# A fused cross-attention and mixture-of-experts layer: the closing loads and stores take four or five neighbouring token rows per partition, and the shared tiles follow in steps of four columns

## What is computed

```python
x = x + xattn(layernorm(x), ctx)        # q, k, v from layernorms, softmax over 361 keys, output product
h = layernorm(x)
shared = gelu(h @ ws1 + bs1) @ ws2 + bs2
aff = softmax(h @ Wr + br)              # 31 experts
vals, idx = top_k(aff, 3)               # a gate for each of the three experts of a token
routed = sum over experts e: gate_e * (gelu(h @ We1[e] + Be1[e]) @ We2[e] + Be2[e])
out = x + shared + routed + h
```

## Time and profile before

| | |
|---|---|
| median of 3 runs | 559.9 us (558.31 to 562.15) |
| the profiled execution, its own time | 565.31 us |
| its span, first to last instruction | 563.7 us |
| TensorE busy | 494.3 us (88%) |
| VectorE busy | 349.2 us (62%) |
| GpSimd busy | 323.2 us (57%) |
| ScalarE busy | 248.2 us (44%) |
| mean granted TensorE clock | 0.958 |
| moved by DMA | 97.53 MB, mean 173 GB/s |

### The profile page before, as it was taken

One profiled execution on the slowest core, in us unless ns is written; L12 is line 12 of the kernel. 1 busy time (PEld: TensorE's weight loads), 2 busy tenths in 40 slices (PEclk: granted clock), 3 DMA queues, 4 the chain that ended last, 5 costly groups with the idle time before them and its releaser, 6 DMA issues.

```text
span 563.7 us, 15096 instructions
## 1 busy us (share of the span) xinstructions
PE 494.3 (88%) x3227; PEld 416.7 (74%) x3228; DVE 349.2 (62%) x1531; ACT 248.2 (44%) x822; POOL 323.2 (57%) x366
## 2 busy tenths in 40 slices
PE   1789888899989988879739999999999999999990
PEld 1777777777777777667528888888888888898760
DVE  2368797878888895443206666666666666663385
ACT  1154566555656556351205444444444444453210
POOL 5032666766775676354106777777777777786000
PEclk9989999999999999787959999999999999999995
DMA  8975677677664422189335887777877887786899
GB/s 248 300 220 161 208 227 251 209 212 225 191 198 137 148 87 87 68 282 375 137 86 90 131 122 125 124 126 127 125 129 126 129 125 126 128 127 74 269 348 315
DMA packets 80618, 97.53 MB, mean 173 GB/s; under 512 B 8401, under 2 KB 65394, under 8 KB 80578
## 3 DMA queue, kind: packets, MB, share of 16 engines
q1 hardware_dynamic: 60146, 70.52, 40.9%
q0 software_dynamic: 19568, 25.88, 27.6%
q10 hardware_dynamic: 864, 0.66, 0.4%
HBM read 55.31 MB, written 41.73 MB: 172 GB/s over the span
## 4 chain that ended last, share of the span: by engine, by line
PE 41%; SPq 10%; issue 6%; POOL 4%; DMA 3%; DVE 3%; ACT 2%; POOLq 0%; DVEq 0%; ACTq 0%
PE bank L1133 15%; PE bank L1122 15%; PE bank L1111 4%; POOL sum L508 3%; SPq L372 2%; SPq L368 2%; DMA w_all<-sum 2%; SPq L399 1%; SPq L398 1%; SPq L373 1%; PE bank L982 1%; SPq L400 1%; DMA sum<-y_sb,token 1%; PE bank L985 1%; PE bank L1032 1%
## 5 line engine op out<-in xcount | busy, mean ns | idle before, releaser
L508 POOL DMA_INDIRECT sum<-y_sb,token x105 | 170.7, 1626 | 73.5 <-issue 63.9
L593 ACT ACTIVATE up<-bank,b_all 128x128 f32<-128x128 f32 x260 | 81.5, 364 | 117.4 <-PE bank L1122 66.8
L1133 PE MATMUL bank<-w_all,up 128*128 x420 | 113.1, 392 | 0.6 <-issue 0.4
L1122 PE MATMUL bank<-xtt,w1b 128*128 128x128 f32 x840 | 112.9, 278 | 0.2
L1122 PEld LDWEIGHTS bank<-xtt,w1b 128*128 128x128 f32 x840 | 102.9, 193 | 3.1 <-issue 2.9
L482 POOL DMA_INDIRECT expert_rows_in<-xt,slot x75 | 74.4, 992 | 35.5 <-issue 31.5
L856 DVE TENSOR_SCALAR y_sb<-bank,gate,inverse 128x256 f32<-128x256 f32 x105 | 57.1, 544 | 42.6 <-PE bank L1133 37.9
L1133 PEld LDWEIGHTS bank<-w_all,up 128*128 128x128 f32 x420 | 71.4, 190 | 10.9 <-issue 1.8
L848 DVE COPY w1b<-w_all 128x512 f32 x105 | 45.2, 430 | 41.4 <-PE bank L1122 37.7
L619 ACT ACTIVATE xtt<-bank 128x256 f32<-128x256 f32 x105 | 40.3, 384 | 59.4 <-PE bank L1111 33.4
L1111 PE MATMUL bank<-ident,xt 128*128 128x128 f32 x210 | 40.7, 276 | 11.9 <-DMA xt<-expert_rows_in 11.9
(11 more groups left out here) (183 smaller groups left out, 904.0 us busy)
## 6 DMA issues: line engine op xcount, KB each, us to landing
xt<-expert_rows_in SPq DMA_DIRECT2D x105, 132.0 KB
w_all<-in_w SPq DMA_DIRECT2D x43, 256.0 KB, 9.7
w_all<-in_ctx SPq DMA_DIRECT2D x32, 288.0 KB
w_all<-sum SPq DMA_DIRECT2D x12, 512.0 KB, 8.9
w_all<-sum SPq DMA_DIRECT2D x9, 384.0 KB, 8.2
sum<-pad_rows SPq DMA_DIRECT2D x1, 3328.0 KB, 12.4
w_all<-in_w SPq DMA_DIRECT2D x1, 3328.0 KB
w_all<-in_x SPq DMA_DIRECT2D x25, 128.0 KB, 3.4
```

The source lines that it names most:

```text
L508: pool.indirect_dma_start(sums[s], bass.IndirectOffsetOnAxis(ap=token[sx][:, 0:1], axis=0), y_sb[sx][:, :], None, compute_op=ALU.add).then ...
L593: ins = act.activation(up[s][:, m * P:m * P + P], up_ps[s][:, m * P:m * P + P], ACT.Gelu, bias=b1_all[:, e, m:m + 1].rearrange("p o n -> p ...
L1122: mm = pe.matmul(up_ps[s][:, m * P:m * P + P], w[:, c * INTER + m * P:c * INTER + m * P + P], xtt[s][:, c * P:c * P + P], start=(c == 0), ...
L1133: mm = pe.matmul(down_ps[s], up[s][:, m * P:m * P + P], w, start=(m == 0), stop=(m == 1))
```

## The change

It has five parts, all of which follow from one new rule: in a group of tiles `lo` to `hi`, partition p now holds the hi - lo neighbouring tokens from lo * 128 + p * (hi - lo) on, so that a group's rows are four (in one group five) neighbouring rows of DRAM for each partition.

1. The layout: `rows_of` is rearranged as "(p k) n -> p k n". A tile t of the shared expert is now the columns `every(t)` of `tok`, 128 columns at a step of 4 (of 5 in one group), where it was 128 neighbouring columns. This holds for the right-hand side of `up_shared`, for the gates in `down_shared`, for the output of `evac_shared` and for the read of `tok` in the closing addition. `up_shared` waits for `h_t_copied` of the whole group.
2. The groups: six of 4, 4, 4, 4, 5 and 4 tiles, where there were seven of 3, 4, 3, 4, 3, 4 and 4. So 18 loads and 6 stores in place of 21 and 7; the bytes are the same. The last group is tiles 8 to 11, where it was tiles 21 to 24.
3. The gates: one transpose of 32 columns per tile (25) in place of 7 of 128 columns, into one row of 3200 columns in 32 partitions; 7 copies on ScalarE in place of 2. The copies alternate between two PSUM banks, so some transposes wait for a copy.
4. The order: copies 1 and 2 and their transposes stand in steps 33 and 34; the last four rounds follow each other after `early(5)`; ScalarE's copies for them stand one gelu earlier (`u == 6`).
5. At the start: `b2_all` is loaded once in place of four times, and one memset goes.

```diff
-GROUPS = [(12, 15), (0, 4), (15, 18), (4, 8), (18, 21), (8, 12), (21, 25)]
+GROUPS = [(12, 16), (0, 4), (16, 20), (4, 8), (20, 25), (8, 12)]
+GATES = [(0, 4), (4, 8), (8, 12), (12, 16), (16, 20), (20, 24), (24, 25)]
...
-        gates_all = sb("gates_all", [P, 28, NE + 1])
-        gates_t = sb("gates_t", [P, 7, P])
+        gates_all = sb("gates_all", [P, TILES, NE + 1])
+        gates_t = sb("gates_t", [NE + 1, TOKENS])
...
+        group_of = {t: g for g in GROUPS for t in range(*g)}
+
+        def every(t):
+
+            lo, hi = group_of[t]
+            return slice(lo * P + t - lo, hi * P, hi - lo)
...
+        def gates_ps(r):
+            lo, hi = GATES[r]
+            return bank[7 if r in (4, 6) else 6][0:NE + 1, 0:(hi - lo) * P]
...
-                return dram[lo * P:hi * P, :].rearrange("(k p) n -> p k n", p=P)
+                return dram[lo * P:hi * P, :].rearrange("(p k) n -> p k n", p=P)
...
-            for q in range(4):
-                pool.dma_start(b2_all[q * 32:q * 32 + NE + 1, :], b2).then_inc(small_in, 16)
+            pool.dma_start(b2_all[:, :], b2).then_inc(small_in, 16)
...
+            def copy_gates(r):
+                lo, hi = GATES[r]
+                act.wait_ge(gates_transposed, r + 1)
+                act.activation(gates_t[:, lo * P:hi * P], gates_ps(r), ACT.Copy).then_inc(gates_t_copied, 1)
+
             for i in STEPS:
                 if i == B + 1:
-                    act.wait_ge(gates_transposed, 4)
-                    act.activation(gates_t[:, 0:4, :].rearrange("p g q -> p (g q)"), bank[6][:, :], ACT.Copy).then_inc(gates_t_copied, 1)
+                    copy_gates(0)
                 step(i)
                 if i == B + 1:
                     gelu_shared(0)
                     gelu_shared(1)
+                    copy_gates(1)
+                if i == B + 2:
+                    copy_gates(2)
             for u in range(2, S_E):
                 gelu_shared(u)
-                if u == 7:
-                    act.wait_ge(gates_transposed, 7)
-                    act.activation(gates_t[:, 4:7, :].rearrange("p g q -> p (g q)"), bank[7][:, 0:3 * P],
-                                   ACT.Copy).then_inc(gates_t_copied, 1)
+                if u == 6:
+                    for r in range(3, len(GATES)):
+                        copy_gates(r)
...
-                dve.tensor_copy(tok[:, :, cut(u)], down_ps[u % 2].rearrange("p (c q) -> p c q", c=2)).then_inc(y_made, 1)
+                dve.tensor_copy(tok[:, :, every(u)], down_ps[u % 2].rearrange("p (c q) -> p c q", c=2)).then_inc(y_made, 1)
...
-                    dve.tensor_tensor(rows, rows, tok[:, :, lo * P:hi * P].rearrange("p c (k q) -> p k c q", q=P),
+                    dve.tensor_tensor(rows, rows, tok[:, :, lo * P:hi * P].rearrange("p c (q k) -> p k c q", q=P),
...
-                pe.wait_ge(h_t_copied, t + 1)
+                pe.wait_ge(h_t_copied, group_of[t][1])
...
-                                       tok[:, c, cut(t)], start=(c == 0), stop=(c == 1))
+                                       tok[:, c, every(t)], start=(c == 0), stop=(c == 1))
...
-                pe.wait_ge(gates_t_copied, 1 if t < 16 else 2)
+                pe.wait_ge(gates_t_copied, min(len(GATES), (group_of[t][1] + 3) // 4))
...
-                pe.matmul(to, gates_t[q:q + NE + 1, t // 4, :], b2_all[q:q + NE + 1, :], start=False, stop=True)\
+                pe.matmul(to, gates_t[:, every(t)], b2_all[:, :], start=False, stop=True)\
...
+            def turn_gates(r):
+                lo, hi = GATES[r]
+                pe.wait_ge(gates_made, hi)
+                if r in (1, 2, 3, 5, 6):
+                    pe.wait_ge(gates_t_copied, {1: 1, 2: 2, 3: 3, 5: 4, 6: 5}[r])
+                for t in range(lo, hi):
+                    mm = pe.transpose(gates_ps(r)[:, (t - lo) * P:(t - lo + 1) * P], gates_all[:, t, :], ident[:, :])
+                mm.then_inc(gates_transposed, 1)
```

More of the change, by code:

```diff
@@ L149, in program @@
         b1_all = sb("b1_all", [P, NE + 1, 2])
-        b2_all = sb("b2_all", [P, D1])
+        b2_all = sb("b2_all", [NE + 1, D1])
         ident = sb("ident", [P, P])
         ones, tri = sb("ones", [P, P], BF16), sb("tri", [P, P], BF16)
-        gates_all = sb("gates_all", [P, 28, NE + 1])
-        gates_t = sb("gates_t", [P, 7, P])
+        gates_all = sb("gates_all", [P, TILES, NE + 1])
+        gates_t = sb("gates_t", [NE + 1, TOKENS])
         iota_slot, iota_e, tile_no = sb("iota_slot", [P, NE]), sb("iota_e", [P, NE]), sb("tile_no", [P, 1])
@@ L266, in program @@
         sum_made, final_made, final_out = sems("sum_made", "final_made", "final_out")
-        MADE = 22
+        MADE = 21
         LATE = 18
@@ L441, in _ @@
                             allow_small_or_imprecise_dtypes=True))
-            const(pool.memset(gates_all[:, 0:TILES, NE:NE + 1], 1.0))
-            k = const(pool.memset(gates_all[:, TILES:28, :], 0.0))
+            k = const(pool.memset(gates_all[:, 0:TILES, NE:NE + 1], 1.0))
             assert k == MADE, k
@@ L800, in _ @@
             dve.tensor_tensor(fold_o1[D2B:D2C, 0:D1], fold_o1[D2B:D2C, 0:D1], bo_row[D2B:D2C, :], ALU.add).then_inc(folds_ready, 1)
-            dve.wait_ge(small_in, 16 * 7)
+            dve.wait_ge(small_in, 16 * 4)
             for i in STEPS[2:]:
@@ L953, in _ @@
             pe.wait_ge(folds_ready, 1)
-            pe.wait_ge(small_in, 16 * 7)
+            pe.wait_ge(small_in, 16 * 4)
             def step(i):
@@ L1042, in up_shared @@
                         mm = pe.matmul(up_ps[s][:, m * P:m * P + P], w1_all[:, NE, c * INTER + m * P:c * INTER + m * P + P],
-                                       tok[:, c, cut(t)], start=(c == 0), stop=(c == 1))
+                                       tok[:, c, every(t)], start=(c == 0), stop=(c == 1))
                 mm.then_inc(up_made, 1)
             def down_shared(u, t, to):
-                s, q = u % 2, 32 * (t % 4)
+                s = u % 2
                 pe.wait_ge(act_made, u + 1)
-                pe.wait_ge(gates_t_copied, 1 if t < 16 else 2)
+                pe.wait_ge(gates_t_copied, min(len(GATES), (group_of[t][1] + 3) // 4))
                 for m in range(2):
                     pe.matmul(to, up[s][:, m * P:m * P + P], w2_all[:, NE, m * D1:(m + 1) * D1], start=(m == 0), stop=False)
-                pe.matmul(to, gates_t[q:q + NE + 1, t // 4, :], b2_all[q:q + NE + 1, :], start=False, stop=True)\
+                pe.matmul(to, gates_t[:, every(t)], b2_all[:, :], start=False, stop=True)\
                   .then_inc(down_made, 1)
@@ L1059, in early @@
                 down_shared(u, u, down_ps[u % 2])
-            def turn_gates(lo, hi, to):
-                pe.wait_ge(gates_made, min(TILES, 4 * hi))
-                for g in range(lo, hi):
-                    pe.transpose(to[:, (g - lo) * P:(g - lo + 1) * P], gates_all[:, 4 * g:4 * g + 4, :].rearrange("p k e -> p (k e)"),
-                                 ident[:, :]).then_inc(gates_transposed, 1)
+            def turn_gates(r):
[6 more added lines that the diff above has]
+                mm.then_inc(gates_transposed, 1)
             for i in STEPS:
@@ L1070, in _ @@
                     pe.wait_ge(shared_in, 32)
-                    turn_gates(0, 4, bank[6])
+                    turn_gates(0)
                 step(i)
@@ L1078, in _ @@
                     early(0)
+                    turn_gates(1)
                 if i == B + 2:
@@ L1081, in _ @@
                     early(1)
+                    turn_gates(2)
             pe.wait_ge(msum_made, TILES)
@@ L1096, in _ @@
             pe.wait_ge(logit_sum, TILES)
-            turn_gates(4, 7, bank[7])
+            for r in range(3, len(GATES)):
+                turn_gates(r)
             for u in range(7, S_E):
```

## The result

Timed in turn on one chip, the kernel took 561.02 us before (median of 4 runs, 558.31 to 562.32) and takes 568.14 us after (4 runs, 567.47 to 570.43). The ratio is 1.014, 95% interval 1.0089 to 1.0192. It is slower by 7.1 us; the forecast was 560.0, no change.

What follows compares the result with a forecast made beforehand. The prediction took loads to bound the close and SP's padding writes the middle. Close +0.35, middle 0, start -0.2 and steps 0 made +0.15 us, on the median of 559.9 a forecast of 560.0 us, range 556.4 to 568.5.

Steps and rivals of the forecast that it cites:

- The read of `tok` at a step of 4: TensorE's `up_shared` reads at a step: 0 us taken from a VectorE row, upper bound a doubling, 0.89 us per tile.
- Rival 2: TensorE reads `tok` at half speed: +5.5 us in the close, +2.7 in the middle, together +8.2, 568.1; chance 0.16.
- The packets and the rate: Closing loads: packets stay at 1 KB and the rate at 348 GB/s, so 0 us gained.
- Rival 1: Closing loads get faster, at 407 GB/s, from four rows in one piece of DRAM: 3.0 us less, 556.9; chance 0.17.
- The groups: Close with the new groups: last group's additions start at 555.4 and end at 559.2, before 558.8; +0.35 us.
- The wait of 0.6 us at the seventh late product: In the close, TensorE's seventh late product waits for the first group's first tile until 532.8, against 532.20 before.
- The gates, `pads_ready` and the middle: New gate round trips delay `pads_ready` to 253.8 to 254.3, SP at 255.6: 1.3 to 1.8 us spare, 0 us cost.
- rival 3: Gate round trips in steps 33 and 34 cost more, `pads_ready` late: with 5 in place of 1.5, +2 us, 562.0; chance 0.06.
- I am wrong if TensorE still works after 553 us: Sign against the forecast in the close, where TensorE was expected to end its late tiles at 549.2.

Runs made afterwards that it cites:

- experiment 1: The kernel after with the layout taken back to 128 neighbouring columns, new groups, transposes, copies and order kept: 563.99 us, ratio 0.9996.
- experiment 2: The kernel before with only the up products of tiles 12 to 23 reading `tok` at a step: 565.37 us at 4, 564.28 at 2, 564.61 at 3.
- Experiment 4: The kernel before with `rows_of` as (p k): 565.97 us, ratio 1.0022; then also with SBUF parts without gaps: 559.56 us, ratio 0.9937.
- with the parts: The kernel before with `rows_of` as (p k) and `part0` to `part2` without gaps between tiles in SBUF: 559.56 us, ratio 0.9937.
- experiment 7: The kernel after with rows in pairs (step 2), parts without gaps, tile 24 its own group: 560.59 us, ratio 0.9932; with tile 24 last: 561.88 us, 0.9955.
- experiment 3: The kernel after with only the up products of late tiles 12 to 24 reading neighbouring columns of `tok`: 563.97 us, ratio 1.0031.
- experiment 6: The kernel after with tiles 8 to 11 before tiles 20 to 24: 567.94 us, ratio 1.0085; the kernel after unchanged beside it: 569.35 us, 1.0112.

## Why the prediction was wrong, point by point

**The step that failed** is "The read of `tok` at a step of 4": "So the low end is 0 and I take that". It took VectorE's reduction of 93 numbers for all reads at a step. TensorE needed 1.88 us in place of 1.00 for eight instructions (experiments 1 and 2), +0.88 us per tile, where the upper bound was 0.89. It did not even hold for VectorE: the closing addition of 1024 columns went from 1.23 to 1.99 us, and the copy into `tok`, which writes at the step, from 0.42 to 0.61. What differs may be the size or the kind of the instruction, or that line 722 takes its 93 numbers three at a time, 31 apart, and so comes back to the same 16 bytes after three numbers; no run here tells these apart. The likelihood was wrong too: a doubling, in the bounds and with a rule of the Trainium skill behind it, got 0.16 because a single row of another engine stood against it.

**Rival 2 is what happened,** in size: 568.1 forecast, 568.14 measured. But it is partly a chance of compensating terms. The sum was +8.2 on a median of 559.9, and measured are +7.1 on one of 561.02. Its +5.5 for the close was +7.8: TensorE's late tiles took 13 x 1.04 = 13.5 us more, not 11.6, because of the gates' weights (0.14 a tile, forecast 0 to 0.3), and the closing addition was 0.75 longer, which I had not counted at all; the last store took 1.25 us less (565.6 - 561.95 = 3.65, against 4.9), with no other store under way beside it. And the first load was issued 7.9 us after the late tiles had begun, not 8.8 as before, which left TensorE 0.9 us more to do behind it. Its +2.7 for the middle did not come in the profiled execution of the result, where idle time went from 11.45 to 0.40 us and no further; in two others it came as some 2.2.

**The packets and the rate: right.** 1 KB and 346 GB/s, against 348. Experiment 4 shows the reason that was argued from the earlier trace rows: with DRAM rows alone the packet stays 1 KB. Rival 1 was thus wrong for this change; its price of 3.0 us was about right for loads that do get faster: in the groups of before, with the parts, the ratio of 0.9937 is 3.5 us, and the close was 4.5 us shorter (40.8 to 36.3). The Trainium skill ("DMA: Bandwidth & Descriptors", Why small descriptors are slow) came by my estimate to 6% for 4 KB packets; measured is 348 against 397 GB/s, 12% of the time, and so nearer to the 14% that I had worked out from the weights of the earlier trace rows.

**The groups: right.** With the layout taken back, the last group's additions started at 555.45 (forecast 555.4) and ended at 559.2 (forecast 559.2); the ratio was 0.9996. The wait of 0.6 us at the seventh late product did not come: not in the kernel after, where TensorE was late itself, and not with the layout taken back, where that product starts at 533.79, a microsecond behind the 532.8 that it was to wait for.

**The gates, `pads_ready` and the middle: right in size, its reason not borne out.** To spare were 1.2 us, forecast 1.3 to 1.8 (0.6 to 0.7 in the four other profiled executions with the early steps of 4); rival 3 did not happen. But the new round trips of gates, which were to use up the difference to 2.9, used none of it where they stand without the steps of 4, in experiment 1:

```profile
253.12 0.18 DVE L829 TENSOR_TENSOR pad_row<-bank,iota_slot 1x31 int32<-1x31 f32 x1
255.96 0.92 SPq L381 DMA_DIRECT2D expert_rows_in<-pad_rows  x1
```

`pads_ready` at 253.3, SP at 256.88: 3.6 us to spare, more than before; in the two runs of experiment 7, with the round trips and steps of 2, it is 3.3 and 1.6. So it varies, but most of what went in the kernel after went with the steps of 4. Wrong as well is how much of the idle time went: forecast were 8 us left.

**Which is the owner of the end:** "I am wrong if TensorE still works after 553 us". It worked until 557.1, or 40.1 us after the first load, where before it was 26.6 us.

So the loss takes two things together. Slow reads of the up products in the order of before cost about half a microsecond of waiting for TensorE (experiment 2; there tile 24 and the gates were flat, so TensorE ended 2.7 us sooner than in the kernel after), and the new groups and their order alone cost nothing (experiment 1). With both, and the smaller slow reads, the close is 7.8 us longer, of which 7.5 go again when the late up products read flat (experiment 3), and 4.0 to 4.2 when only the last two groups change places (experiment 6). The order had moved TensorE's last tile to the group before the last, which is harmless while the loads are late, and puts 4.4 us of additions behind TensorE once it is the last.

## What to carry to other kernels

Before a matmul or an addition reads at a step, count how many wanted numbers share 16 bytes: two float32 (a step of 2) were free here, one (a step of 4) cost TensorE 88% and VectorE 44 to 62%, and a small instruction of another kind is no evidence for a big one. A longer run in DRAM gives longer packets only if the SBUF side has no gaps either. When the order of groups is chosen, put the tile that the slowest engine makes last into the last group, so that a slip of that engine costs one addition and not a whole group (4 us of the close here, of which the medians show 1 to 2).

## What the hardware showed that was not expected

- The cost of a step is not one of being strided: 125, 127, 182, 235 and 241 ns per instruction of 128 columns at steps 1 to 5. A LDWEIGHTS of 32 rows by 128 columns took 311 ns at a step of 4, 199 in pairs and 193 without a step (means over the whole span). Since it overlaps the matmuls, TensorE lost only 0.14 us a tile by two of them.
- Packets of 3 to 4 KB moved 397 GB/s on average and 416 at the best, of 2 KB 390, of 1 KB 344 to 356 (means over stretches of 6 to 22 us). Most of the gain is there at 2 KB.
- In the middle the granted clock differs from execution to execution. Busy time from 230 to 260 and from 260 to 295 us, before:

```profile
230.00:260.00 30.00, 24.16 (x111) 19.02 (x110) 12.64 (x63) 12.47 (x42) 16.54 (x23) 0.72 0.68 242
260.00:295.00 35.00, 23.12 (x121) 16.88 (x120) 6.47 (x21) 6.16 (x19) 4.88 (x9) 0.80 0.49 164
```

And after:

```profile
230.00:260.00 30.00, 25.70 (x121) 20.34 (x121) 12.93 (x64) 12.41 (x38) 17.05 (x24) 0.89 0.79 282
260.00:295.00 35.00, 33.62 (x159) 26.70 (x158) 9.60 (x31) 9.61 (x28) 4.99 (x9) 1.00 0.41 133
```

The clock is at 0.72 and 0.80 of full speed where TensorE is busy for 24.2 of 30 and 23.1 of 35 us, that is at the lower of its two levels (1.2 and 2.4 GHz) for part of the time, and at 0.89 and 1.00 where it is busy for 25.7 and 33.6. It looks like a matter of idle time, but the second execution of the kernel after speaks against so simple a reading:

```profile
230.00:260.00 30.00, 25.86 (x117) 20.22 (x118) 12.75 (x63) 13.09 (x42) 16.51 (x23) 0.80 0.76 271
260.00:295.00 35.00, 34.37 (x146) 26.55 (x147) 9.09 (x27) 8.42 (x25) 4.85 (x9) 0.93 0.44 142
```

TensorE is busy for as long and longer here, at 0.80 and 0.93. In the execution with 0.89 and 1.00 the twelve early tiles, each slower by 1.04 us, fitted into 11 us of idle time; in this one TensorE came some 2.2 us late. So the clock may be what decides whether they fit; that is argued from these rows, not tried.
